# A 16x16 triangular inverse per lane: moving the systems to lanes and back by VectorE's 32x32 block transposes instead of TensorE products

## The reference, cut to what matters

```python
def step(S, inps):
    qi, ki, vi, bi = inps
    pred = jnp.einsum('bhkv,bhk->bhv', S, ki)
    S = S + bi[..., None, None] * ki[..., :, None] * (vi - pred)[..., None, :]
    o = jnp.einsum('bhkv,bhk->bhv', S, qi)
    return (S, o)
S0 = jnp.zeros((b, H, DK, DV), x.dtype)
_, o = jax.lax.scan(step, S0, (qt, kt, vt, bt))
```

## Time and profile before

| | us |
|---|---|
| median of 3 runs | 720.32 |
| lowest, highest | 718.02, 723.84 |
| the profiled execution | 717.71 |
| its span | 715.9 |
| busy: TensorE / VectorE / ScalarE / POOL | 587.2 / 448.5 / 257.6 / 96.9 |
| mean granted clock of TensorE | 0.87 |

### The profile page before, as it was taken

How to read it: one execution, slowest core, us unless ns; L and a number is a source line. 1 busy time by engine, 2 the same in 40 slices (tenths; PEclk the granted TensorE clock), 3 DMA queues, 4 the chain that set the end, 5 groups by cost and what they waited for, 6 DMA issues and landing times.

```text
span 715.9 us, 17173 instructions
## 1 busy us (share of the span) xinstructions
PE 587.2 (82%) x7376; PEld 395.0 (55%) x7376; DVE 448.5 (63%) x1125; ACT 257.6 (36%) x571; POOL 96.9 (14%) x140
## 2 busy tenths in 40 slices
PE   1687980877799999796699769968689999999994
PEld 1544650467698867656498647854444444444442
DVE  4956495888868444847846972874665555555552
ACT  1365530654340635353434244243322222222221
POOL 2454471410000102100100010210200000000000
PEclk9988995875569999898758889997879999999998
DMA  9995003000000000000000410000212634344321
GB/s 333 320 369 222 1 20 99 0 2 2 2 2 5 4 2 2 2 2 1 1 3 4 136 55 2 5 1 1 66 30 66 173 88 112 85 105 114 88 60 29
DMA packets 19084, 46.78 MB, mean 65 GB/s; under 512 B 3809, under 2 KB 8545, under 8 KB 18753
## 3 DMA queue, kind: packets, MB, share of 16 engines
q1 hardware_dynamic: 18368, 45.43, 20.8%
q10 hardware_dynamic: 640, 0.26, 0.2%
HBM read 43.32 MB, written 2.36 MB: 64 GB/s over the span
## 4 chain that ended last, share of the span: by engine, by line
PE 60%; DVE 25%; ACT 4%; POOL 4%; SPq 2%; issue 2%; DMA 2%; DVEq 0%; POOLq 0%
PE psum L760 8%; PE psum L755 8%; PE psum L765 8%; PE psum L596 4%; PE psum L718 3%; PE psum L692 3%; PE psum L721 3%; PE psum L562 3%; PE psum L727 2%; POOL rstd L963 2%; SPq L410 2%; DVE yr L1302 2%; PE psum L623 2%; PE psum L466 2%; PE psum L681 2%
## 5 line engine op out<-in xcount | busy, mean ns | idle before, releaser
L942 ACT ACTIVATE arena<-psum 128x512 f32<-128x512 f32 x68 | 40.6, 597 | 133.3 <-PE psum L755 125.5
L1380 DVE TENSOR_TENSOR arena<-psum,arena 128x512 f32<-128x512 f32 x64 | 44.2, 691 | 62.2 <-PE psum L760 60.4
L765 PE MATMUL psum<-arena,wed_sb 128*128 128x512 f32 x128 | 67.0, 606 | 0.0
L783 ACT ACTIVATE arena<-psum 128x512 f32<-128x512 f32 (+1 forms) x72 | 34.3, 501 | 66.4 <-PE psum L562 40.8
L1385 DVE TENSOR_TENSOR arena<-arena 128x512 f32<-128x512 f32 x64 | 44.3, 692 | 14.7 <-PE psum L765 14.6
L562 PE MATMUL psum<-arena 32*64 32x128 f32 x1024 | 42.3, 322 | 9.9 <-DVE XA L1295 5.2
L562 PEld LDWEIGHTS psum<-arena 32*64 32x64 f32 x1024 | 36.2, 162 | 14.8 <-DVE XA L1295 5.9
L962 POOL TENSOR_TENSOR ve<-ss,eps_rms 128x4 f32<-128x4 f32 x16 | 4.3, 270 | 287.6 <-ACT yr L834 201.5
L765 PEld LDWEIGHTS psum<-arena,wed_sb 128*128 128x128 f32 x128 | 24.9, 194 | 31.6 <-issue 24.2
L760 PE MATMUL psum<-yT,weu_sb 128*128 128x512 f32 x68 | 37.3, 632 | 3.9 <-DVE arena L1380 3.9
L755 PE MATMUL psum<-yT,weg_sb 128*128 128x512 f32 x68 | 36.9, 626 | 2.2 <-ACT yr L783 2.2
(11 more groups left out here) (284 smaller groups left out, 1221.2 us busy)
## 6 DMA issues: line engine op xcount, KB each, us to landing
arena<-shares SPq DMA_DIRECT2D x64, 256.0 KB, 4.0
arena<-in_ctx_t SPq DMA_DIRECT2D x16, 514.0 KB, 8.4
arena<-in_ctx_z SPq DMA_DIRECT2D x16, 512.0 KB, 9.4
XA<-in_x SPq DMA_DIRECT2D x1, 1024.0 KB, 4.9
zlast<-in_ctx_last SPq DMA_DIRECT2D x4, 256.0 KB, 16.6
X<-x_mid SPq DMA_DIRECT2D x2, 512.0 KB, 4.5
weg_sb<-in_we_gate SPq DMA_DIRECT2D x2, 512.0 KB, 6.4
weu_sb<-in_we_up SPq DMA_DIRECT2D x2, 512.0 KB, 7.2
```

The costliest lines, as they stand in the source:

```text
L765: pe.matmul(x3, wed_sb[:, (p - 1) % (NPAIR + 1), :], act_a[pr], start=(p == 0), stop=False, skip_group_check=True).then_inc(x_down[pr], 1)
L783: return act.activation(out_, in_, ACT.Copy, scale=scale)
L942: act.activation(act_g[pr], banks[4 * pr + 2 * (n % 2)], ACT.Silu).then_inc(x_silu[pr], 1)
L1380: dve.tensor_tensor(act_gu[pr], banks[4 * pr + 1], act_g[pr], ALU.mult).then_inc(x_gu[pr], 1)
```

## The change

Four things are done. (1) `AC` is laid out system by system, so that the 16 entries of a system lie side by side (`chunks_of`). (2) The products of `to_lanes` and of `from_lanes` are gone from TensorE; VectorE's block transpose takes `AC` to `XL` as the first instruction of `inv0` (it writes the elements of a matrix's column 64 elements apart), and a second one takes `XL` to a new view `back` at the end of `inv3`. A block transpose turns each block of 32 partitions by 32 elements by itself; a lane is then another set of partition and column than before, but the layout after both is what the old pair gave. (3) ScalarE's four copies for each u read `back` in SBUF (elements of one system 64 elements apart) and wait on `l_inv` from VectorE; before they read PSUM. (4) The mask of the triangle is no more applied to the turned matrices: a 16-column mask `strict` is made once, POOL multiplies it with `nbeta` in stage `sq` into `nbm` (128x512, eight times in all), and the last instruction of `ext` multiplies by `nbm` instead of `nbeta`. The 31 memsets that made `below` are gone, five small instructions make `strict`.

```diff
@@ -246,19 +246,21 @@
         work = [flat(t) for t in yr[0:NU]] + [flat(pcT)[:, u * 2 * GW:(u + 1) * 2 * GW] for u in range(NU)]
         sq = work
         AC = [work[pr * NU] for pr in range(2)]
+        back = [work[pr * NU + 1] for pr in range(2)]
         WT = [work[g][:, 0:GW] for g in range(NG)]
         osq = [work[g][:, 0:GW] for g in range(NG)]
         P1 = [work[g][:, GW:2 * GW] for g in range(NG)]
         gate = [work[g][:, 0:GW] for g in range(NG)]
         prod = rowv[:, 0:2, :].rearrange("p i c -> p (i c)")
-        below = rowv[:, 2:4, :].rearrange("p i c -> p (i c)").rearrange("p (r m) -> p r m", r=C16)
-        take = carve(sb("small", [P, 256])[:, :])
+        take = carve(sb("small", [P, 272])[:, :])
         eye64, tril, tri32 = take((T,)), take((T,)), take((S,))
         chunk = [take((1,)) for j in range(NC)]
         first, second = take((1,)), take((1,))
         head_of = [take((1,)) for par in range(2)]
         head_is = take((H,))
         own_head = take((HQ,))
+        strict = take((C16,))
+        nbm = [KQ[g][:, 3 * GW:4 * GW].rearrange("p (n i) -> p n i", i=C16) for g in range(NG)]
         NH = GT * 2 * H
         hsum, hve, hrs = ([flat(t) for t in pair] for pair in (s1[0:NU], p1[0:NU], p1T[0:NU]))
         route = []
@@ -367,7 +370,7 @@
 
         def chunks_of(pr, u):
 
-            return AC[pr].rearrange("p (i n) -> p n i", i=C16)[:, u * NB:(u + 1) * NB, :]
+            return AC[pr].rearrange("p (n i) -> p n i", i=C16)[:, u * NB:(u + 1) * NB, :]
 
         def quarter(t, q):
 
@@ -563,26 +566,6 @@
                                 "p (c q) -> p c q", c=2), KT[g][par][rows_, c0:c0 + T], both, start=True, stop=True)
                 return last
 
-            def to_lanes(pr):
-
-                a = AC[pr].rearrange("p (i n) -> p i n", i=C16)
-                for i in range(C16):
-                    for s2 in range(2):
-                        rows_ = slice(s2 * T, (s2 + 1) * T)
-                        c0 = pr * 4 * 512 + i * T
-                        last = pe.matmul(psum[rows_, c0:c0 + T], a[rows_, i, :], ident[rows_, rows_], start=True, stop=True)
-                return last
-
-            def from_lanes(bank, pr, u):
-                xl = XL[pr].rearrange("p (m c) -> p m c", m=C16)
-                for m in range(C16):
-                    for s2 in range(2):
-                        rows_ = slice(s2 * T, (s2 + 1) * T)
-                        lane0 = s2 * T + u * NB
-                        last = pe.matmul(bank[rows_, m * NB:(m + 1) * NB], xl[rows_, m, :], ident[rows_, lane0:lane0 + NB],
-                                         start=True, stop=True)
-                return last
-
             def two_parts(t, tt, h):
 
                 return t[:, tt * 2 * D:(tt + 1) * 2 * D].rearrange("p (c n) -> p c n", c=2)[:, :, h * DK:(h + 1) * DK]
@@ -638,13 +621,6 @@
                         else:
                             pe.wait_ge(g_diag[u], pi * 4 + q)
                         gram(bank, g, q).then_inc(g_mm[u], 1)
-                    elif kind == "lin" and u == 0:
-                        for k in range(NU):
-                            pe.wait_ge(s_ext[k], pi + 1)
-                        to_lanes(pr).then_inc(l_mm, 1)
-                    elif kind == "lout":
-                        pe.wait_ge(l_inv, pi + 1)
-                        from_lanes(b1, pr, u).then_inc(l_omm[u], 1)
                     elif kind[0] == "a":
                         half = int(kind[2])
                         pe.wait_ge(l_out[u], pi + 1)
@@ -881,8 +857,8 @@
                         copy(chunks_of(pr, u),
                              GA[g].rearrange("p (n c) -> p n c", c=T)[:, :, 0:C16], chunk[0]).then_inc(s_ext0[u], 1)
                     elif kind == "lout":
-                        act.wait_ge(l_omm[u], pi + 1)
-                        lanes = b1.rearrange("p (m n) -> p n m", m=C16)
+                        act.wait_ge(l_inv, pi + 1)
+                        lanes = back[pr].rearrange("p (r n) -> p n r", r=C16)[:, u * NB:(u + 1) * NB, :]
                         for j in range(NC):
                             last = copy(TT[g].rearrange("p (n c) -> p n c", c=T)[:, :, j * C16:(j + 1) * C16], lanes, chunk[j])
                         last.then_inc(l_out[u], 1)
@@ -1014,6 +990,11 @@
                                            qkv[g][:, :, 2 * D:3 * D].rearrange("p j (h e) -> p j h e", h=H),
                                            bc(beta[g][:, :, :].unsqueeze(3), [P, GT, H, DK]),
                                            ALU.mult).then_inc(q_vb, 1)
+                        if l == 0 and u == 0:
+                            pool.wait_ge(strict_made, 1)
+                        pool.wait_ge(q_nb, i + 1)
+                        pool.tensor_tensor(nbm[g], bc(nbeta[g][:, :, :].rearrange("p j h -> p (j h)").unsqueeze(2), [P, NB, C16]),
+                                           bc(strict.unsqueeze(1), [P, NB, C16]), ALU.mult).then_inc(q_nbm, 1)
                     elif kind == "n2":
                         pool.wait_ge(m_ss, i + 1)
                         rsqrt(st, g, ss[g][:, 0:GT], GT, eps_rms, m_rr)
@@ -1216,12 +1197,11 @@
             st.after(dve.tensor_scalar(tril[:, 0:T // 2], tri32, first, None, ALU.mult))
             dve.tensor_scalar(tril[:, T // 2:T], tri32, second, first, ALU.mult, ALU.add).then_inc(masks_made, 1)
             dve.wait_ge(masks_made, 1)
-            for m in range(C16):
-                last = dve.memset(below[:, m, :], 0.0)
-            st.after(last)
-            for m in range(1, C16):
-                last = dve.memset(below[:, m, 0:m], 1.0)
-            st.after(last)
+            st.after(dve.tensor_scalar(strict, tril[:, 0:C16], chunk[0], None, ALU.mult))
+            for j in range(1, NC):
+                st.after(dve.scalar_tensor_tensor(out=strict, in0=tril[:, j * C16:(j + 1) * C16], scalar=chunk[j], in1=strict,
+                                                  op0=ALU.mult, op1=ALU.add))
+            dve.tensor_scalar(strict, strict, -1.0, 1.0, ALU.mult, ALU.add).then_inc(strict_made, 1)
 
             for kind, l, pr in STEPS:
                 pi = l * 2 + pr
@@ -1274,7 +1254,7 @@
                     elif kind == "sq":
                         dve.wait_ge(q_silu, pi * 4 + 2 + u + 1)
                         dve.tensor_scalar(beta[g][:, :, :], th[g][:, :, :], 1.0, None, ALU.add).then_inc(q_beta, 1)
-                        dve.tensor_scalar(nbeta[g][:, :, :], th[g][:, :, :], -1.0, -1.0, ALU.mult, ALU.add)
+                        dve.tensor_scalar(nbeta[g][:, :, :], th[g][:, :, :], -1.0, -1.0, ALU.mult, ALU.add).then_inc(q_nb, 1)
                         dve.wait_ge(q_sq, i + 1)
                         st.after(dve.tensor_reduce(hsum[pr][:, u * NH:(u + 1) * NH],
                                                    sq[g].rearrange("p (h e) -> p h e", e=DK), AX.X, ALU.add))
@@ -1301,18 +1281,15 @@
                         for j in range(1, NC):
                             st.after(dve.scalar_tensor_tensor(out=mine, in0=ga[:, :, j * C16:(j + 1) * C16], scalar=chunk[j],
                                                               in1=mine, op0=ALU.mult, op1=ALU.add))
-                        dve.tensor_tensor(mine, mine, bc(nbeta[g][:, :, :].rearrange("p j h -> p (j h)").unsqueeze(2),
-                                                         [P, NB, C16]), ALU.mult).then_inc(s_ext[u], 1)
+                        dve.wait_ge(q_nbm, i + 1)
+                        dve.tensor_tensor(mine, mine, nbm[g], ALU.mult).then_inc(s_ext[u], 1)
                     elif kind[:3] == "inv" and u == 0:
                         part = int(kind[3])
                         xl = XL[pr].rearrange("p (r j m) -> p r j m", r=C16, j=NC)
                         if part == 0:
-                            dve.wait_ge(l_mm, pi + 1)
-                            if pi >= 2:
-                                for k in range(NU):
-                                    dve.wait_ge(l_omm[k], pi - 1)
-                            lanes = psum[:, pr * 4 * 512:(pr * 4 + 2) * 512].rearrange("p (m j r) -> p r j m", m=C16, j=NC)
-                            st.after(dve.tensor_tensor(xl, lanes, bc(below.unsqueeze(2), [P, C16, NC, C16]), ALU.mult))
+                            for k in range(NU):
+                                dve.wait_ge(s_ext[k], pi + 1)
+                            st.after(dve.transpose(xl.rearrange("p r j m -> p m j r"), AC[pr].rearrange("p (n i) -> p i n", i=C16)))
                         for i_ in range(*PIVOTS[part]):
                             rest = C16 - 1 - i_
                             shape = [P, rest, NC, i_]
@@ -1323,7 +1300,8 @@
                         if part == len(PIVOTS) - 1:
                             for j in range(NC):
                                 last = dve.memset(XL[pr][:, j * C16:j * C16 + (C16 - 1) * (T + 1) + 1:T + 1], 1.0)
-                            last.then_inc(l_inv, 1)
+                            st.after(last)
```

(1 more changed line is left out.)

9 lines of the change are left out of this document (5 added, 4 removed).

## The result

The changed kernel takes 731.5 us (median of 6, 727.0 to 732.3), the kernel before on the same chip 721.5 (median of 6, 718.0 to 729.2): a ratio of 1.010 (95% interval 1.006 to 1.015). It is slower by 1%, where 706 was forecast; the range 695 to 720 doesn't hold it. The profiled execution took 727.0 us, of which 725.2 are span, at a mean granted clock of 0.83; before it was 717.7, 715.9 and 0.87. It is the fastest of the six, so the profiles lie 9.3 us apart and the medians 10.0.

The account below looks back on a forecast made before the run. The chain, 60% TensorE and 25% VectorE, was taken to bound the kernel, shortenable only in the two delta attention layers. -7.2 + 5.3 - 5.2 - 5.7 + 0.4 + 1.0 = -11.4 from 717.7 gave 706 us, range 695 to 720.

Parts of the forecast that it names:

- ext and way in: From `ext` to the first pivot: shorter instructions -3.35, VectorE's idle time -2.7, first transpose +0.9; together -5.15 us.
- place 1: Layer 0, stream A: way in, way out and B's `to_lanes` gain, a slow `ah1` costs 3.3; sum -7.2 us.
- place 2: Layer 0, A's `otr` to B's `ah0`: without `from_lanes` of B as cover TensorE's clock falls, +5.3 us.
- the clock staying at 0.5 through A's block products: Layer 0, stream A: without B's `to_lanes` the clock doesn't rise, so `ah1` gets slow, +3.3 us.
- Way out: Inverse to block products, layer 0, A: transpose and copies at 0.60 each take 4.7 us for 6.97, -2.3.
- The rival on it: ScalarE's `lout` copies pay for strided reads, 1.18 us instead of 0.60 each: +8.1, so 714.4 us; chance 0.2.
- place 4: Layer 1, stream B: `ext` gives 2.8, `inv0` costs 0.9 more, `from_lanes` (3.85) goes; -5.7 us.
- The first stretch: From the start to A's `ah0` in layer 0: -7.1 us forecast.
- `wt` and the carry steps: Layer 0, stream A, behind the block products: the carry steps start on the low clock, +1.0 us.
- the slower rival: Layer 0, from A's `wt` on, the clock stays down: +16.5 us, total 723 us; chance 0.07.
- Place 3: Layer 1, stream A: the way in gains as in layer 0, the way out nothing; -5.2 us.
- POOL: Head norm of A, layer 0: VectorE's two-input operations wait beside POOL's mask products, +0.4 us.

Follow-up runs that it names:

- f3: e1 with 22 filler products instead of 6 in front of each `otr`: 714.0 us, ratio 0.989.
- e1: The changed kernel with the second block transpose writing `back` by stride, so that ScalarE reads runs: 716.8 us, ratio 0.990.
- e4: The kernel before with `AC` laid out system by system, `to_lanes` kept and reading by stride: 730.2 us, ratio 1.004.
- h3: The changed kernel, reads strided, with g2's 64-column products and 22 fillers at A's `otr` of layer 0: 724.5 us, ratio 1.004.
- g2: g1 with the 32 products of B's `to_lanes` in layer 0 put back on `ident`, result unused: 708.6 us, ratio 0.979.
- g4: g1 with the mask multiplied on VectorE and POOL's eight products gone: 716.0 us, ratio 0.989.
- g1: e1 with 22 fillers instead of 6 in front of A's `otr` in layer 0 alone: 710.4 us, ratio 0.982.
- g3: g1 without POOL's eight mask products, the triangle's mask left out: 709.3 us, ratio 0.983.
- b1: The kernel before with 22 filler products instead of 6 in front of each `otr`: 740.5 us, ratio 1.026.
- e2: e1 with POOL's product of `nbeta` and mask moved from `sq` to `gram0`: 723.2 us, ratio 0.998.
- f2: The changed kernel with 16 fillers before A's block products in both layers and 22 at each `otr`: 730.5 us, ratio 1.013.

## Why the prediction was wrong

*ext and way in* were right in size (-5.15 forecast for both, -5.3 measured at place 1), and so was place 2: +5.3 forecast, +6.2 in the changed kernel, and 5.6 us come back in f3 by filling the gap. The forecast of the clock staying at 0.5 through A's block products was right too.

*Way out* is the step that failed first, the price of ScalarE's strided reads: "I take 0.60 a copy as now". Measured are 1.08 from copy to copy, and 1.18 and 1.16 for one, the bound that the prediction gave. That term alone turned a gain into a loss (e1, 14.7 us between medians); with reads in runs the way out is as forecast, 17.6 us from the first pivot to A's block products for 20.0 before (-2.4, forecast -2.3). L1203 beside L1208 was a bad witness: another engine, and 128 elements, whose 278 ns are the same as other short instructions'. The nearer row was ScalarE's own strided write, 1182 ns. The rule of the Trainium skill that the prediction weighed and set aside (SBUF — State Buffer, the note on "cachelines") holds for these reads; for TensorE's weights in e4, read 64 bytes apart, no price was to be seen (3.74 us for 3.68).

*The rival on it had the cause and half the price*: +8.1 forecast, 14.7 between medians, 16 in h3 against g2. It counted four copies at places 1 and 3, but the second group's block products follow at once and wait for eight (8.60 in the chain). It left out B in layer 0 (+3.9 in h3 against g2). At place 4 it had 3.5, and took the wait for a wait alone: behind 2.17 us without work TensorE's clock was down, and it fell once more later in the stretch, which shows +8.3.

*The first stretch* came to -3.5 where -7.1 was forecast. Of the 3.6, the slow copies are 1.7 (the way out gave 0.6 of its 2.3). The rest is that `ext` began 2.4 us later than before, where 0.4 was allowed for POOL. Two things were late there, and either would have done: POOL's products cost 2.1 at full clock (g4 against g1), and the second qkv projection took 7.23 us for 5.53, which without them comes to 1.7 (g3, 39.1 for 37.4). The clock of the projection isn't of the change's making: in b1 and e4, up to there the kernel before, it took 6.96 and 7.05.

*Place 1*, `wt` and the carry steps: "+1.0". Without `to_lanes` of B nothing lifted the clock until A's `o` or later, and in some profiles not then (e2, f2, g4): +2.7 in the profile where +1.2 was forecast. That was the slower rival's mechanism; it came in part. Its witness against, the 3 us in which the clock came back, was the very work that the change takes out. That this work lifts the clock there is shown by g2; what in it does so isn't.

*Place 3*, -5.2: -0.9 in e1 and -3.9 in g2, from B's `o` on. The gain is made between `ext` and the pivots, but A's first `gram` started at the low level in e1 (310.68, 3.49 us for what took 1.90), and the chain goes over B's projection and ScalarE's order (B's `sq` stands ahead of A's `lout`), which doesn't get earlier with A. That stood in the chain of before, right ahead of the copies:

```profile
346.75 6.52 PE psum L623 x16
354.17 1.89 ACT pcT L865 x2
```

The prediction saw the copies and didn't ask what they waited for: a term of 5.2 us, of which 0.9 came in e1. *Place 4*, -5.7: -3.3 in e1, -4.6 in g2; the size was 1.1 to 2.4 us too large.

*POOL*, +0.4: 2.1 where TensorE doesn't hide it (g4 against g1), 0.6 where it does in part (e1 against g3). It held up one-input instructions, which the prediction hadn't counted.

Together, between profiles: -11.4 was forecast and +10.1 came. Of these 21.5 us, 10.2 are the strided reads (changed kernel against e1; the medians say 14.7). The other 11.3 are in e1: 2.7 before A's `ah0` (1.0 of it lost ahead of the qkv projection, the rest POOL and the projection), 1.2 in the next two stretches, 5.7 at place 3 and behind it, 2.4 at place 4, less 0.6 at the end (0.1 is rounding). How much of these is clock and how much is gain that the other stream covers was not separated.
